# Attention image tower: two of four causal masks on low query rows taken by a minimum on VectorE, and the row maxima turned by ordinary products

## What is computed

```python
h = (abs(conv(gray(x), scharr_x)) + abs(conv(gray(x), scharr_y))) / 2
n = layernorm(h)
Q = (n @ W_dq) @ W_uq;  K = (n @ W_dkv) @ W_uk;  V = (n @ W_dkv) @ W_uv   # 16 heads of 16
scores = Q @ K.T / sqrt(16);  scores = where(k <= q, scores, -inf)         # causal
h = h + (softmax(scores) @ V) @ W_o
h = h + layernorm(h) @ sign(weight).T
```

## Time and profile before

| what | value |
|---|---|
| median of 3 launches | 418.94 us (417.73 to 421.58) |
| the profiled launch | 420.82 us |
| its span, first to last instruction | 419.0 us |
| mean granted TensorE clock | 0.975 of 2.4 GHz |
| instructions in the span | 10082 |

### The profile page before, as it was taken

How to read it: one execution, slowest core, us unless ns; L and a number is a source line. 1 busy time by engine, 2 the same in 40 slices (tenths; PEclk the granted TensorE clock), 3 DMA queues, 4 the chain that set the end, 5 groups by cost and what they waited for, 6 DMA issues and landing times.

```text
span 419.0 us, 10082 instructions
## 1 busy us (share of the span) xinstructions
PE 379.0 (90%) x3667; PEld 261.4 (62%) x3667; DVE 290.5 (69%) x551; ACT 239.7 (57%) x410; POOL 168.3 (40%) x359
## 2 busy tenths in 40 slices
PE   2967867788999999999999999999999998979985
PEld 0432445556676767676777767676767675757663
DVE  3225543778777877787878686878786868767751
ACT  2125343766675848494848485767674756353631
POOL 8000050547363626263636363636452432321221
PEclk9977996999999999999999999999999999989999
DMA  6984978688787878869696969798666261610001
GB/s 191 213 175 130 225 186 256 184 206 214 228 220 231 247 210 230 231 170 265 164 265 152 253 173 251 187 232 201 180 170 176 61 181 59 197 58 28 7 22 52
DMA packets 72283, 74.14 MB, mean 177 GB/s; under 512 B 6403, under 2 KB 66091, under 8 KB 72235
## 3 DMA queue, kind: packets, MB, share of 16 engines
q1 hardware_dynamic: 70506, 72.71, 65.0%
q10 hardware_dynamic: 1729, 0.80, 0.8%
HBM read 51.98 MB, written 21.04 MB: 174 GB/s over the span
## 4 chain that ended last, share of the span: by engine, by line
PE 63%; DMA 15%; SPq 8%; DVE 6%; issue 3%; ACT 2%; POOL 1%; POOLq 0%; ACTq 0%; DVEq 0%
PE bank L1020 13%; PE bank L1151 7%; PE bank L1084 7%; PE bank L1113 6%; SPq L344 5%; DMA gray_padded<-gray 4%; PE bank L1034 4%; DMA x_sb<-in_x 4%; DMA qk_parts<-parts 4%; PE bank L1069 3%; PE bank L1050 3%; PE bank L1013 3%; PE bank L1086 3%; PE bank L1115 3%; PE bank L1130 3%
## 5 line engine op out<-in xcount | busy, mean ns | idle before, releaser
L662 ACT ACTIVATE probs<-bank 128x1024 f32<-128x1024 f32 x64 | 65.1, 1017 | 49.4 <-PE bank L1115 48.5
L856 DVE TENSOR_REDUCE top<-bank 128x4 f32<-128x1024 f32 x64 | 78.0, 1219 | 21.2 <-PE bank L1086 21.1
L866 DVE TENSOR_TENSOR bank<-bank,cap_kq 128x512 f32<-128x512 f32 x64 | 44.7, 698 | 27.1 <-PE bank L1130 24.6
L1084 PE MATMUL bank<-k_st,q_st 96*128 96x256 bf16 x256 | 46.8, 277 | 6.4 <-DMA k_st<-qk_parts 4.9
L1113 PE MATMUL bank<-q_st,k_st 99*128 99x256 bf16 x256 | 47.1, 278 | 1.7 <-DMA q_st<-top_rows 1.7
L1151 PE MATMUL bank<-probs,v_ring 128*32 128x256 f32 x512 | 41.3, 394 | 4.8 <-DVE rest L849 3.2
L861 DVE TENSOR_REDUCE top<-bank 128x4 f32<-128x512 f32 x64 | 41.6, 650 | 0.0
L667 ACT ACTIVATE probs<-bank 128x512 f32<-128x512 f32 x64 | 38.0, 594 | 2.0 <-DVE bank L866 1.9
L481 POOL TENSOR_SCALAR var<-mv 128x2 f32<-128x2 f32 x16 | 3.6, 225 | 84.4 <-DVE mv L907 84.4
L1115 PE MATMUL bank<-mask_kq,ident_bf 128*128 128x256 bf16 x128 | 35.6, 278 | 0.0
L873 DVE STREAM_TRANSPOSE u<-bank 128x256 f32<-128x256 f32 x64 | 28.7, 448 | 9.7 <-PE bank L1154 4.5
(11 more groups left out here) (109 smaller groups left out, 766.3 us busy)
## 6 DMA issues: line engine op xcount, KB each, us to landing
x_sb<-in_x SPq DMA_DIRECT2D x16, 768.0 KB, 5.4
rows<-gray_padded SPq DMA_DIRECT2D x48, 256.0 KB
qk_parts<-parts SPq DMA_DIRECT2D x48, 256.0 KB, 3.2
q_st<-qk_parts SPq DMA_DIRECT2D x96, 128.0 KB, 3.4
k_st<-qk_parts SPq DMA_DIRECT2D x96, 128.0 KB, 3.4
gray_padded<-gray SPq DMA_DIRECT2D x16, 258.0 KB, 3.8
out_dram<-z SPq DMA_DIRECT2D x15, 256.0 KB, 2.9
rows<-gray_padded SPq DMA_DIRECT2D x32, 24.0 KB
```

The lines of the kernel that those rows point to most:

```text
L662: nc.scalar.activation(probs[:, g, :, 0:S], ps_k0, ACT.Exp, scale=SCALE).then_inc(exp0_done, 1)
L856: nc.vector.tensor_reduce(top[:, 1, g // 2, :, g % 2], ps_hi, AX.X, ALU.max, negate=True).then_inc(max_hi_done, 1)
L866: nc.vector.tensor_tensor(ps_k1, ps_k1, cap_kq[:, :].unsqueeze(1).to_broadcast([P, G, P]), ALU.min).then_inc(capped, 1)
L1084: nc.tensor.matmul(ps_hi[:, i, :], q[:, hh, P:S], k[:, hh, :], start=(i == b * two), stop=False, skip_group_check=True)
```

## The change

Three edits. First, in head groups 1 and 2 the low query-major scores get no mask product: `lo_scores` issues its four products alone, each closed in itself. VectorE then takes a minimum of the bank with `cap_qk` (a 128x128 f32 table, -3e38 where forbidden, +3e38 elsewhere) in place, in a new step `cap_lo`, before `max_lo`. Second, VectorE's order changes with it: in the second quarter `cap_lo(1)` stands where `max_lo(1)` stood and `max_lo(1)` comes behind `turn_attn`; in the third `cap_lo(2)` comes between `max_hi(2)` and `invert`. GpSimd sets up the new table at the start, ahead of `drawn`. Third, `turn_max` uses an ordinary product with the bf16 identity into f32 in PSUM instead of a transpose into bf16.

```diff
+LO_MIN = (1, 2)
...
-        ps_mt = bank[:, 5, :].bitcast(BF16)
+        ps_mt = bank[:, 5, :]
...
+                pool.affine_select(out=cap_qk[:, :], in_=cap_qk[:, :], compare_op=ALU.is_ge, fill=MASK,
+                                   base=0, pattern=[[-1, P]], channel_multiplier=1).then_inc(drawn, 1)
...
+            pool.memset(cap_qk[:, :], -MASK).then_inc(cleared, 1)
...
             def max_lo(n, g):
-                dve.wait_ge(lo_done, NG * n + g + 1)
+                if g in LO_MIN:
+                    dve.wait_ge(lo_capped, len(LO_MIN) * n + LO_MIN.index(g) + 1)
+                else:
+                    dve.wait_ge(lo_done, NG * n + g + 1)
...
+            def cap_lo(n, g):
+                dve.wait_ge(lo_done, NG * n + g + 1)
+                nc.vector.tensor_tensor(ps_lo, ps_lo, cap_qk[:, :].unsqueeze(1).to_broadcast([P, G, P]),
+                                        ALU.min).then_inc(lo_capped, 1)
...
                     max_hi(i, 1)
-                    max_lo(i, 1)
+                    cap_lo(i, 1)
                 if i == 1:
                     turn_values(0, 0)
                     rest_of_gray(4)
                 if live(i - 2):
                     turn_attn(i - 2, 1)
+                if live(i):
+                    max_lo(i, 1)
...
                     max_hi(i, 2)
+                    cap_lo(i, 2)
...
                 need(pe, max_lo_done, NG * n + g)
+                if g in LO_MIN:
+                    for i in range(G):
+                        hh = g % 2 + 2 * i
+                        last = nc.tensor.matmul(ps_lo[:, i, :], q[:, hh, 0:P], k[:, hh, 0:P],
+                                                start=True, stop=True)
+                    last.then_inc(lo_done, 1)
+                    return
...
-                    last = nc.tensor.transpose(ps_mt[0:PARTS * HALF, t * P:(t + 1) * P],
-                                               top_parts[:, t, :, :].rearrange("p c h -> p (c h)"),
-                                               ident_bf[:, :])
+                    last = nc.tensor.matmul(ps_mt[0:PARTS * HALF, t * P:(t + 1) * P],
+                                            top_parts[:, t, :, :].rearrange("p c h -> p (c h)"),
+                                            ident_bf[:, :], start=True, stop=True)
```

More of the change, by code:

```diff
@@ L100, in build @@
         ones = sb("ones", [PARTS * HALF, 2 * S], BF16)
+        cap_qk = sb("cap_qk", [P, P])
         cap_kq = sb("cap_kq", [P, P])
@@ L261, in build @@
         capped = sem("capped")
+        lo_capped = sem("lo_capped")
         exp0_done = sem("exp0_done")
@@ L444, in draw_masks @@
             def draw_masks():
-                pool.wait_ge(cleared, 7)
+                pool.wait_ge(cleared, 8)
                 for m in (ident, ident_bf):
@@ L545, in _ @@
             pool.memset(v_ring[:, :, :, :, DK:VW], 1.0).then_inc(ones_set, 1)
-            pool.wait_ge(drawn, 2 * TAPS + 5)
+            pool.wait_ge(drawn, 2 * TAPS + 6)
             pool.wait_ge(ones_set, 1)
@@ L557, in _ @@
                     sum_edges(i + 2)
+                if live(i + 2):
                     scale_x(i + 2)
@@ L1208, in keep_warm @@
                     nc.tensor.matmul(bank[:, 5, :], ident_bf[:, :], mask_qk[:, :, :], start=True, stop=True)
-            pe.wait_ge(drawn, 2 * TAPS + 5)
+            pe.wait_ge(drawn, 2 * TAPS + 6)
             keep_warm(36)
```

## The result

| what | before | after |
|---|---|---|
| median of 16 launches each, same chip | 418.0 us | 415.79 us |
| ratio after to before, 95% interval | | 0.9944, 0.992 to 0.9968 |
| the profiled launch, and its span | 420.82 us, 419.0 us | 414.74 us, 412.7 us |

The change gains 0.56%, 2.3 us. The ratios leave out launches over 1.5% above the fastest of their kernel, so a ratio need not be the quotient of two medians. The two profiled launches lie 6.1 us apart: that of before was 2.8 us over its median, that of after 1.1 us under. So the gain has to be looked for in parts of the run that repeat, and those are the images in the middle. A second measurement, further down, gave 0.9912 (0.9873 to 0.9951).

The account below looks back on a forecast made before the run. TensorE's stream was taken to bound the middle: 4.84 us from images 3 to 13, 0.44 from image 14 and 0.22 from image 15 make 5.5 us. From 418.94 that gives 413.4, named 414.0 us; range 410.5 to 418.5.

Parts of the forecast that it names:

- faster by over 1%: Whole run: a time under about 415 us, given a chance of 0.66.
- In the middle: Images 3 to 13, eleven periods of 21.67 us: each 0.44 us shorter, 4.84 us in all.
- What bounds the kernel: From 115 to 353 us TensorE almost alone sets the time; up to 114.3 us DMAs and SP's queue do.
- Nothing is lost. So I take 0.22 us for each mask.: TensorE, second and third quarter: the f32 product behind each removed mask moves up by all 0.22 us, 0.44 an image.
- load exposed: Rival, TensorE behind the removed masks: the f32 weight load shows, gain 0.17 us a mask, 415.3 us; chance 0.12.
- The walk along the engines: One image followed step by step on VectorE and GpSimd: the added work hides in waits, about 0.15 us spare at `compress`.
- The minima on VectorE: `cap_lo`, second and third quarter: 0.70 us each, hidden in the waits before `add_z` and `add_y`, 0.6 us left at the latter.
- slower at `compress`: Rival: VectorE's transpose comes late for `compress` in thirteen images, 4.3 us more, 423.5 us; chance 0.08.
- The turn at nothing: `turn_max` by ordinary products: counted as 0, with a gain of up to 6.4 us kept as a small chance.
- something else holds the rate: Rival, middle images: DMA loads may come too late for a faster TensorE, 418.5 us; chance 0.12.
- Images at the ends: Images 0 to 2 give nothing, image 14 gives 0.44 us, image 15 0.22; cost at the start 0, at most 0.3.
- The clock: Rival, start: the fall of the granted clock at 64.0 us may not come, 2.5 us less, 411.5 us; chance 0.18.

Follow-up runs that it names:

- the reordering: Changed kernel with ScalarE's copy_xt(i + 2) ahead of scale_colors(i + 4) from the third iteration on: ratio 0.9902 to the kernel before, an image 21.29 us.
- turn_only: Kernel before with only the turn of the maxima changed to ordinary products into f32, masks as before: ratio 0.9981, an image 21.67 us.
- the repeated pair: Changed kernel and the same with the maxima turned by transposes, both measured a second time side by side: ratios 0.9912 and 0.9928.
- before_xt_first: Kernel before, both TensorE masks in place, with copy_xt ahead of scale_colors on ScalarE: ratio 0.9986, an image 21.67 us.
- min_g2: Changed kernel with the minimum in the third head group alone, the second group's mask product back on TensorE: ratio 0.9993, an image 21.50 us.
- after_again: The changed kernel, unaltered, measured a second time: ratio 0.9912 to the kernel before.
- mask_again: Changed kernel with the maxima turned by transposes as before, measured a second time: ratio 0.9928 to the kernel before.
- mask_only: Kernel before with only the masks changed, the maxima still turned by transposes: ratio 0.9885, an image 21.43 us.

## Why the prediction was right, and where its size was off

The median after came out at 415.79 us, within the range of 410.5 to 418.5 and 1.8 us over the 414.0 named. The direction and the mechanism were right. The gain was not: 2.3 us instead of 5.5, so what was held likeliest, faster by over 1%, did not come about. That the number came so near is partly luck. The forecast started from 418.94 us and rounded up to 414.0 because the median of three might be low; it was high, the sixteen launches give 418.0, and 5.5 us off that would have been 412.5. In the middle the forecast was 4.84 us, and the two profiles of after show 2.8 and 2.2. The third group's mask gave 1.8 and the second's 2.3, together 4.1; the waits for ScalarE's copy took back 0.9 and 1.0, the late DMA of image 5 0.3 and 0.7. Another 0.1 went in image 13, where `turn_x` starts 0.08 us late with the copy behind or first.

- **What bounds the kernel.** Right. TensorE's stream sets the middle, and what is taken off it shows in the period of an image.
- **"Nothing is lost. So I take 0.22 us for each mask."** This is the first term mis-sized. It measured 0.21 us in the second group and 0.16 in the third. The one place of the trace that was used as proof, L1130 followed by L1013, has f32 products of 128 columns behind it, whose loads take 0.14 us. It stands for the second group, and there it held. Behind the third stands `compress`, f32 products of 256 columns with loads of 0.19 us. The *start* of the first product was predicted right in both. The delay comes one product later. The trace of before had a sign of it that was not looked for: behind the two short products of the turn (L1168) stand f32 products of 256 columns, 27 times, and there too the first pair is wide apart, 0.320 us instead of 0.215:

```profile
213.48 0.48 PE L1020 MATMUL bank<-w_out,a_t 128*128 128x256 f32 x1
213.80 0.38 PE L1020 MATMUL bank<-w_out,a_t 128*128 128x256 f32 x1
```

  The prediction also says that no other place of before tests whether a product starts before its load is complete. Many do: the second L1097 starts at 206.876, and its load runs from 206.819 to 206.917.
- **The rival "load exposed"** gave 0.17 us a mask. The size was right for one group of two, the place for none: it had the first f32 product 0.11 us behind the last short one, and that distance is 0.055 in both. The Trainium skill, "TensorE: Matmul & The Clock Gate", section LDWEIGHTS, puts the load of 128 columns at columns/1.2 ns, an estimate of 107 ns. The trace has 140 and 190 ns for f32 loads of 128 columns here, so the measurement decides, and the agreement with 0.17 is luck of the subtraction.
- **The walk along the engines** is where the second loss was missed: 0.44 us an image asks every engine to deliver 0.22 to 0.44 us earlier. VectorE and GpSimd were walked and ScalarE was not. It had 6.7 us idle an image, but a busy chain of 4.5 us just ahead of `copy_xt`, and before the change it was in time by only 0.07 us. This cost about 0.14 us in six and seven of the eleven images, 0.9 and 1.0 us in the two profiles, shown by the reordering.
- **The minima on VectorE.** Right at each place: 0.69 us, the wait before `add_z` gone, 0.66 us left before `add_y` (0.6 forecast), `compress` in time. The rival "slower at `compress`" fell, with the period unchanged when both masks were kept.
- **The turn at nothing.** Right in the middle, by turn_only and the repeated pair.
- **The rival "something else holds the rate"**, by DMA, was right once. The 12 KB load of the maxima's rows for image 5 comes late: TensorE waits 0.2 us before, 0.5 and 0.9 us in two profiles of after, 1.0 us with the copy first, and not at all in the profiles of before_xt_first, turn_only and min_g2. By the length of that quarter (5.45 us before, 0.40 more than in the other images; 5.51 and 5.91 after, 0.67 and 1.07 more than 4.84), 0.27 and 0.67 us of the changed kernel's gain go back there.
- **Images at the ends.** Image 14 gave 0.28 us (17.23 to 16.95), 0.44 was forecast. From the first scores of image 3 to those of image 14 it took 238.86 us before, 236.08 and 236.63 in two profiles of after: 2.8 and 2.2 us, with the late loads in them. With image 14 it is 2.5 to 3.1 us, beside 2.3 us by the times (1.3 to 3.3). For image 15 and the start the profiles scatter by more than the term.
- **The clock.** It fell to 0.50 at 26.4, 36.7, 64.0 and 374.6 us before and at 25.9, 56.6, 73.7 and 370.7 us after. A clock that falls elsewhere was named as a sign of being wrong. But it fell at other places from profile to profile in kernels of either kind, and no gain or loss can be put down to the change. The Trainium skill, "TensorE: Matmul & The Clock Gate", Part 4 (PE-mode transpose), says that the full clock doesn't engage for transposes. No run here tests that: the 64 transposes stand among 3667 products, and turning them into ordinary products gave 0.9981 (0.9952 to 1.001).

## What to carry to other kernels

When a stream that sets the pace is to run 0.4 us an image ahead, list every wait of that engine, with the slack of each releaser, not only the releasers that the change touches: an engine 30% idle can be busy without a gap just where it is needed. When a long product that hid a load is taken out, look in the trace for a place with the same pair of instructions (type, columns and length of the load), and read the distances one product further than the first. And where launches scatter by more than the gain, measure the period of a loop in the trace, image by image: without waits it repeats here to 0.01 us, and it separated 0.07 from 0.17 us, which twelve launches of each kernel could not.

## What the runs showed that was not expected

- **A load that is hidden once is late once later.** After four products of 128 columns 0.055 us apart, the first f32 product starts on time, and the second 0.056 us late where its load takes 0.19 us, 0.007 us late (0.115 for 0.108) where it takes 0.14. In the first case that load starts 0.056 us after the first product instead of 0.002. What holds the load back was not tried.
- **The granted clock falls, or does not, behind the same stretch.** At the end of image 13 there is a stretch in which TensorE is busy 1.50 of 3.40 us. In after_again the clock stays, in mask_again it falls to 0.50 (1.2 GHz). Busy time by stretch, first after_again:

```profile
344.80:348.20 3.40, 1.50 (x25) 0.99 (x24) 3.01 (x8) 2.36 (x5) 2.09 (x8) 1.00 0.00 0
348.20:351.60 3.40, 3.40 (x27) 2.53 (x27) 2.38 (x4) 2.63 (x5) 1.06 (x2) 1.00 0.16 44
```

and mask_again:

```profile
348.10:351.50 3.40, 1.50 (x25) 0.99 (x23) 2.95 (x6) 2.36 (x4) 2.08 (x8) 1.00 0.00 0
351.50:354.90 3.40, 3.40 (x17) 2.43 (x15) 2.06 (x4) 2.36 (x5) 1.23 (x2) 0.50 0.28 78
```

  From the first scores of image 14 to the end it took 64.06 us in the first and 67.07 in the second, where the fall lasted 10.2 us. (The first has a fall of 3.4 us later, at 370.6, that the second lacks.) Eight of the twelve experiments' profiles had a fall there, in kernels with ordinary products and with transposes, and neither of the two first profiles had one. The two above are not the same kernel. Of the same kernel, mask_only fell for 3.4 us and mask_again for 10.2, with 64.97 and 67.07 us to the end. These 2.1 us between two launches are about the whole gain. What decides whether and for how long the clock falls was not tried.
- **The late load of image 5** comes in eleven of the fourteen profiles at the same image, and TensorE goes on at 163 to 168 us into the run. It was longest, 1.0 us, in one of those with the shortest image. What holds the DMA up there stays open.
